# A decoder layer on one core: exponentials left unnormalised until the head output, and their high halves made by ScalarE

## The reference

```python
q = rmsnorm(x @ w_qa, q_norm_w) @ w_qb           # 16 heads, 128 + 64 rotary
kv = rmsnorm(kv_c, kv_norm_w) @ w_kvb            # 16 heads, keys and values of 128
scores = einsum('blhd,bmhd->bhlm', q, k) * scale # causal mask
attn = softmax(scores, axis=-1)
out = einsum('bhlm,bmhd->blhd', attn, v)
x = x + out.reshape(B, L, H * DV) @ w_o
```

## Time and profile before

| | us |
|---|---|
| median of 3 runs | 1166.24 (1164.35 to 1167.4) |
| profiled execution, its own time | 1167.31 |
| its span, first to last instruction | 1165.5 |
| PE busy | 957.6 (82%) |
| DVE busy | 963.2 (83%) |
| ACT busy | 643.6 (55%) |
| POOL busy | 249.7 (21%) |

### The profile page before, as it was taken

The page is one execution under the profiler, slowest core; times in us unless marked ns, Lnnn a source line. Parts: engine busy times, 40 slices in busy tenths (PEclk is TensorE's granted clock), DMA queues, the critical chain, the costliest instruction groups (busy, mean ns, idle before and its releaser), DMA issues.

```text
span 1165.5 us, 17748 instructions
## 1 busy us (share of the span) xinstructions
PE 957.6 (82%) x5622; PEld 546.8 (47%) x5640; DVE 963.2 (83%) x2902; ACT 643.6 (55%) x1437; POOL 249.7 (21%) x268
## 2 busy tenths in 40 slices
PE   0446567889999999999999999999978655559997
PEld 0324333554554555555555555555535444435553
DVE  5767748999888988998998988988968898857885
ACT  1446546666555656656656656666513675753442
POOL 1036522122112112212212212112100113221211
PEclk9769789999999999999999999999989888769999
DMA  9300004534433446443436433335364530002434
GB/s 346 145 1 1 10 8 85 93 76 80 94 67 78 81 78 154 84 74 78 88 77 151 77 70 68 68 63 136 71 212 109 146 103 6 1 0 37 80 85 91
DMA packets 247661, 98.19 MB, mean 84 GB/s; under 512 B 221832, under 2 KB 233096, under 8 KB 247056
## 3 DMA queue, kind: packets, MB, share of 16 engines
q1 hardware_dynamic: 247568, 97.06, 36.6%
HBM read 36.06 MB, written 7.34 MB: 37 GB/s over the span
## 4 chain that ended last, share of the span: by engine, by line
DVE 48%; PE 34%; ACT 7%; issue 6%; DMA 3%; POOL 2%; SPq 0%; DVEq 0%; ACTq 0%; POOLq 0%
PE bank L1964 8%; PE bank L1912 5%; DVE bank L1541 4%; DVE arena L1558 4%; PE bank L1858 4%; PE bank L1949 4%; DVE arena L1565 4%; DVE arena L797 3%; PE bank L1891 3%; DVE arena L715 2%; DVE arena L717 2%; DMA arena<-arena 2%; DVE arena L681 2%; DVE arena L1572 2%; DVE arena L1525 2%
## 5 line engine op out<-in xcount | busy, mean ns | idle before, releaser
L1241 ACT ACTIVATE arena<-bank,arena 128x128 f32<-128x128 f32 (+3 forms) x256 | 134.3, 525 | 108.2 <-DVE arena L1541 106.7
L1964 PE MATMUL bank<-arena 128*128 128x512 f16 x768 | 180.3, 383 | 1.9 <-DVE arena L1591 1.9
L1565 DVE SCALAR_TENSOR_TENSOR arena<-arena 128x128 f16<-128x128 f32 (+3 forms) x256 | 144.3, 564 | 9.1
L1541 DVE CUSTOM_DVE_ANT_0 bank<-bank,maskb,scal 128x128 f32<-128x128 f32 (+3 forms) x256 | 141.4, 552 | 12.1 <-PE bank L1937 11.6
L1949 PE MATMUL bank<-arena 128*128 128x512 f16 (+3 forms) x768 | 119.7, 308 | 33.6 <-DVE arena L1572 24.6
L1912 PE MATMUL bank<-arena 128*128 128x512 f16 x576 | 137.2, 384 | 0.0
L1949 PEld LDWEIGHTS bank<-arena 128*128 128x128 f16 x768 | 72.8, 100 | 92.9 <-issue 46.4
L1558 DVE TENSOR_SCALAR arena<-arena 128x128 f16<-128x128 f32 (+3 forms) x256 | 109.0, 426 | 7.3 <-DVE arena L1550 0.3
L1964 PEld LDWEIGHTS bank<-arena 128*128 128x128 f16 x768 | 74.0, 99 | 82.9 <-issue 6.0
L1087 POOL TENSOR_TENSOR arena<-arena 128x512 f32<-128x512 f32 x32 | 45.3, 1415 | 308.7 <-ACT arena L1261 308.5
L1261 ACT ACTIVATE arena<-bank 32x512 f32<-32x512 f32 x128 | 75.2, 588 | 30.9 <-PE bank L1891 29.6
(11 more groups left out here) (200 smaller groups left out, 1892.8 us busy)
## 6 DMA issues: line engine op xcount, KB each, us to landing
arena<-arena SPq DMA_TRANSPOSE x308, 2.7
arena<-in_L_attn_w_qb SPq DMA_DIRECT2D x1, 4608.0 KB, 21.0
arena<-in_x SPq DMA_DIRECT2D x4, 1024.0 KB, 6.0
arena<-in_L_attn_w_o SPq DMA_DIRECT2D x1, 4096.0 KB, 31.4
arena<-in_fside_BxS2xS SPq DMA_DIRECT2D x4, 1024.0 KB, 8.2
arena<-in_L_ffn_w SPq DMA_DIRECT2D x8, 512.0 KB, 7.9
out<-arena SPq DMA_DIRECT2D x16, 256.0 KB, 2.4
arena<-in_x SPq DMA_DIRECT2D x12, 256.0 KB, 2.9
```

The costliest lines, as they stand in the source:

```text
L1241: act.activation(pf(k), banks[S_BANKS[G % 3]][:, 0:n].rearrange("p (t c) -> p t c", c=P), ACT.Exp, bias=NB[:, k:k + 1], scale=-1.0, accum_ ...
L1541: dve.tensor_tensor_reduce(s, s, maskb[:, L - n:L], nsc_exp, 3e38, ALU.add, ALU.min, NB[:, (g & 3):(g & 3) + 1]).then_inc(s_max, 1)
L1565: dve.scalar_tensor_tensor(out=ph_part(k, 1), in0=pf(k), scalar=R4[:, k:k + 1], in1=ph_part(k, 0), op0=ALU.mult, op1=ALU.subtract).then_in ...
L1964: last = pe.matmul(banks[Y_BANK][:, :], ot(gp, a, k, (q & 3) * P, P), wo(b, gp * GH + k), start=(k == 0 and n == 0), stop=(k == GH - 1 and ...
```

## The change

- `exps` keeps all 8 row sums of a pair; the exponentials stay unnormalised.
- `probs_hi` moves to ScalarE, right behind `exps` of the same group, as a copy times 4096. `probs_lo` stays on VectorE.
- `row_scale` becomes one reciprocal of four columns for each head.
- The reciprocals of a head lie one per partition (the query row), while the head's output has the queries along its columns. So they are stored to DRAM (`store_sums`, 2 KB) and loaded back spread over all 128 partitions (`spread_sums`, 256 KB) on SP's queue.
- `out_norm` on VectorE multiplies the head output in PSUM by them, in place, ahead of `out_hi`.
- Two output banks, 3 and 7, by the parity of the head. `values` waits for `out_lo` of two heads earlier. The prepared tile's product, which had bank 7, now goes to bank 3.
- The orders on the engines are changed: `out_hi(2i-2)` stands behind `qn_hi_` of group 0, `out_hi(2i-1)` behind `rope_hi` (even pairs, group 5) or at group 6 (odd), and `out_lo(2i-1)` at group 6, ahead of `qn_lo_(2i+2)`, or at group 7. `prep_mm` and what hangs on it stand a group later. `values(i, 0)` waits for `cf_made` in the pairs that prepare a tile.
- `XT` shares the memory of `XN`, `square_out` that of `CF`.

```diff
+    rc_dram = nc.dram_tensor("reciprocals_of_row_sums", (B * H, P * TB), fp32, kind="Internal").ap()
...
-        XT = take(D)
+        RB = take(2 * L)
...
-        NB, SUM, RC, R4 = (small[:, 20 + 4 * k:24 + 4 * k] for k in range(4))
+        NB, SUM, RC = small[:, 20:24], small[:, 24:32], small[:, 32:40]
...
-        S_BANKS, T_BANK, O_BANK, Y_BANK, Q_BANK, R_BANK, P_BANK = (0, 1, 2), 2, 3, 4, 5, 6, 7
+        S_BANKS, O_BANKS, Y_BANK, Q_BANK, R_BANK, P_BANK = (0, 1, 2), (3, 7), 4, 5, 6, 7
...
+            return RB[:, h * L:(h + 1) * L].rearrange("p (q t) -> p t q", t=TB)
...
-                if not (n == TB):
-                    sp.wait_ge(xn_made, n)
+                sp.wait_ge(xn_lo, n)
...
+            def store_sums(Hd):
+
+                sp.wait_ge(s_rc, Hd + 1)
+                sp.dma_start(rc_dram[Hd].rearrange("(q t) -> q t", t=TB),
+                             RC[:, (Hd & 1) * TB:(Hd & 1) * TB + TB]).then_inc(rc_out[Hd & 1], 16)
+
+            def spread_sums(Hd):
+
+                sp.wait_ge(rc_out[Hd & 1], 16 * (Hd >> 1) + 16)
+                if Hd >= 2:
+                    sp.wait_ge(o_nrm, Hd - 1)
+                sp.dma_start(RB[:, (Hd & 1) * L:(Hd & 1) * L + L],
+                             rc_dram[Hd].partition_broadcast(P)).then_inc(rc_in[Hd & 1], 16)
 
             def turn_rows(n):
...
-                    if i % 2 == 0 and g == 3 and i // 2 + TB < NT:
+                    if i % 2 == 0 and g == 4 and i // 2 + TB < NT:
                         turn_keys(i // 2 + TB)
-                    if i % 2 == 0 and g == 4 and i // 2 + TB < NT:
+                    if i % 2 == 0 and g == 5 and i // 2 + TB < NT:
                         turn_latents(i // 2 + TB)
+                    if g in (3, 7):
+                        store_sums(2 * i + (g >> 2))
+                    if g == 5:
+                        spread_sums(2 * i)
+                    if g == 1 and i > 0:
+                        spread_sums(2 * i - 1)
                     turn_probs(i, g)
                     if g == 3 and i % 2 == 0 and i // 2 + 5 < NT:
                         load_xt(i // 2 + 5)
@@ -1052,6 +1082,7 @@
                         if g == 7:
                             reload_xa(i // 8)
                     if i == NPAIR - 1 and g == 7:
+                        spread_sums(2 * i + 1)
                         first_loads(sp)
             later_sync(sp)
 
...
-                    if (j, g) == (0, 2):
+                    if (j, g) == (0, 3):
                         if prep is not None:
                             prep_norm(prep[0])
-                    if (j, g) == (0, 3):
                         if not last:
...
+            def probs_hi(i, g):
+
+                k, G = g & 3, 8 * i + g
+                act.wait_ge(s_exp, G + 1)
+                if not (i == 0 and g < 4):
+                    act.wait_ge(pt_in[k], 16 * (2 * i + (g >> 2)))
+                act.activation(ph_part(k, 0), pf(k), ACT.Copy, scale=PSCALE).then_inc(s_hi, 1)
...
-                act.wait_ge(pv_mm, Hd + 1)
-                act.activation(ot(gpar, 0, slot, 0, L), banks[O_BANK][:, :], ACT.Copy).then_inc(o_hi, 1)
+                act.wait_ge(o_nrm, Hd + 1)
+                act.activation(ot(gpar, 0, slot, 0, L), banks[O_BANKS[Hd & 1]][:, :], ACT.Copy).then_inc(o_hi, 1)
...
                 for g in range(8):
                     exps(G + g, g)
+                    probs_hi(i, g)
                     if (j, g) == (0, 0):
                         qn_hi_(2 * i + 1, 1)
-                    if (j, g) == (0, 1):
+                        if not first:
+                            out_hi(2 * i - 2)
+                    if (j, g) == (0, 2):
                         if prep is not None:
                             prep_squares(prep[0])
                     if (j, g) == (0, 3):
                         if not last:
                             rope_swap(i + 1)
+                    if (j, g) == (0, 4):
                         if prep is not None:
                             prep_scale(prep[0])
-                    if (j, g) == (0, 4):
-                        if not first:
-                            out_hi(2 * i - 1)
                         if not last:
                             qn_hi_(2 * i + 2, 0)
                     if (j, g) == (0, 5):
                         if not last:
                             rope_hi(i + 1, 1 - j)
+                        if not first:
+                            out_hi(2 * i - 1)
+                    if (j, g) == (0, 6):
                         if prep is not None:
                             prep_cn(*prep)
-                    if (j, g) == (0, 7):
-                        out_hi(2 * i)
                     if (j, g) == (1, 0):
                         qn_hi_(2 * i + 1, 1)
+                        out_hi(2 * i - 2)
                     if (j, g) == (1, 2):
                         if not last:
                             rope_swap(i + 1)
                     if (j, g) == (1, 3):
                         if not last:
                             qn_hi_(2 * i + 2, 0)
-                    if (j, g) == (1, 4):
-                        if not first:
-                            out_hi(2 * i - 1)
                     if (j, g) == (1, 5):
                         if not last:
                             rope_hi(i + 1, 1 - j)
                     if (j, g) == (1, 6):
+                        out_hi(2 * i - 1)
                         if ahead is not None:
                             prep_hi(ahead)
-                    if (j, g) == (1, 7):
-                        out_hi(2 * i)
...
+            def row_scale(Hd):
+
+                h = Hd & 1
+                dve.wait_ge(s_exp, 4 * Hd + 4)
+                if Hd >= 2:
+                    dve.wait_ge(rc_out[h], 16 * (Hd >> 1))
+                dve.reciprocal(RC[:, h * TB:h * TB + TB], SUM[:, h * TB:h * TB + TB]).then_inc(s_rc, 1)
...
+                                         scalar=PSCALE, in1=ph_part(k, 0), op0=ALU.mult,
...
+            def out_norm(Hd):
+
+                h = Hd & 1
+                dve.wait_ge(pv_mm, Hd + 1)
+                dve.wait_ge(rc_in[h], 16 * (Hd >> 1) + 16)
+                o = banks[O_BANKS[h]].rearrange("p (t q) -> p t q", t=TB)
+                dve.tensor_tensor(o, o, rb(h), ALU.mult).then_inc(o_nrm, 1)
...
                     if (j, g) == (0, 0):
                         if not first:
-                            row_scale(G - 1, 7)
-                            probs_hi(i - 1, 7)
+                            row_scale(2 * i - 1)
                             probs_lo(G - 1, 7)
+                            out_norm(2 * i - 2)
+                    if (j, g) == (0, 1):
+                        probs_lo(G + 0, 0)
+                        if not first:
                             out_lo(2 * i - 2)
-                    if (j, g) == (0, 1):
-                        row_scale(G, 0)
-                        probs_hi(i, 0)
-                        probs_lo(G, 0)
                         if started(i - 5):
                             add_y(i - 5)
                         qn_lo_(2 * i + 1, 1)
                     if (j, g) == (0, 2):
-                        row_scale(G + 1, 1)
-                        probs_hi(i, 1)
                         probs_lo(G + 1, 1)
+                    if (j, g) == (0, 3):
+                        probs_lo(G + 2, 2)
                         if prep is not None:
                             prep_rope(prep[0], prep[2])
                             prep_var(prep[0])
-                    if (j, g) == (0, 3):
-                        row_scale(G + 2, 2)
-                        probs_hi(i, 2)
-                        probs_lo(G + 2, 2)
-                        if prep is not None:
-                            prep_srq(prep[0])
-                            prep_rope_sum(prep[0])
                     if (j, g) == (0, 4):
-                        row_scale(G + 3, 3)
-                        probs_hi(i, 3)
+                        row_scale(2 * i)
                         probs_lo(G + 3, 3)
                         if not last:
                             rotate(i + 1)
                         if prep is not None:
+                            prep_srq(prep[0])
+                            prep_rope_sum(prep[0])
+                    if (j, g) == (0, 5):
+                        probs_lo(G + 4, 4)
+                        if not first:
+                            out_norm(2 * i - 1)
+                        if prep is not None:
                             prep_split(prep[0])
-                    if (j, g) == (0, 5):
-                        row_scale(G + 4, 4)
+                    if (j, g) == (0, 6):
+                        probs_lo(G + 5, 5)
                         if not first:
...
-                        probs_hi(i, 4)
-                        probs_lo(G + 4, 4)
-                    if (j, g) == (0, 6):
-                        row_scale(G + 5, 5)
-                        probs_hi(i, 5)
-                        probs_lo(G + 5, 5)
```

(40 more changed lines are left out.)

47 lines of the change are left out of this document (16 added, 31 removed).

## The result

The changed kernel takes 1210.3 us (median of four runs, 1209.51 to 1211.02) against 1165.5 for the kernel before: a ratio of 1.038, interval 1.0365 to 1.0401. The forecast was 1183 us and at most 1202: the sign was right, but the loss that it forecast (17 us) was less than half of what came (45).

What follows compares the result with a forecast made beforehand. The prediction took PE as the bound, with the chain through DVE and ACT in pairs 0 to 3. Its terms summed to +17 us on the profiled 1167.3, 1184, so 1183 us for the median; range 1155 to 1202.

Steps and rivals of the forecast that it cites:

- pairs 0 to 5: First six pairs: the chain per pair about 20.5 us against 21.1, so -3 us (-8 to +2).
- pairs 6, 10, 14, 18, 22: Even pairs with a tile, index not a multiple of 4: 23.9 us each, together -2 us (-5 to +2).
- pairs 8, 12, 16, 20: Even pairs whose projection also waits for `out_lo(2i-1)`: 25.85 us each, together +4 us (0 to +8).
- pairs 24, 26, 28, 30: Late even pairs without a tile: 23.6 or 21.65 us against 19.55, together +12 us (+6 to +15).
- clock: TensorE's clock falling after stalls in pairs 8, 12, ..., 28: six chances of 1.7 us, half taken, +5 us (0 to +10).
- all outside the walk's pairs: End of the walk, where `out_norm` lengthens the last head by 0 to 2 us: +1 us.
- The chain: End of even pairs: `out_hi` behind `rope_hi`, with `out_lo` ahead of `qn_lo_`, makes the next scores wait; period 23.9 against 24.25 us.
- the old wait: `values(i, 0)` waiting for `out_lo` of the head before: a 1.8 us stall that two output banks remove.
- The shared buffers and the moved preparation steps cost nothing more: Shared memory and later preparation of a tile: no added cost, since earlier users are done a group or more before.
- by the same walk: Following an even pair's engine operations from its start in the diff's orders; applied to pairs 0 to 5: about 20.5 us.
- PE stays the bound and all stalls go: Faster rival, over the whole walk: the 24.6 us of waits and some 3 us in first pairs go, 1139 us; chance 0.16.
- The third rival: Transposes or reciprocals land late, holding up ACT's exponentials: 0.3 us for each of 64 heads, 1203 us; chance 0.10.

Runs made afterwards that it cites:

- p_pool_held: The changed kernel with only GpSimd's multiplication by the sines held, in pairs with a tile, until VectorE's key part is done: 1209.7 us, ratio 1.037.
- a_qn_first: The changed kernel with `qn_lo_(2i+2)` ahead of `out_lo(2i-1)` on VectorE in group 6 of even pairs: 1199.2 us, ratio 1.028.
- d_kr_early: The changed kernel with the tile's key part (`prep_srq`, `prep_rope_sum`) ahead of `rotate` on VectorE in group 4 of even pairs: 1179.9 us, ratio 1.012.
- o_before_tail_late: The kernel before with one part of the change: key part behind the rotation, the tile's scaling, split and turns a group later: 1182.6 us, ratio 1.015.
- g_all: The changed kernel with three swaps: key part ahead of rotation, `qn_lo_` ahead of `out_lo`, `out_hi` ahead of `rope_hi`: 1154.5 us, ratio 0.991.
- e_dense_rb: The changed kernel with `out_norm` reading the spread reciprocals without the step of four words (values wrong, same work): 1211.8 us in one execution.
- The last version: g_all with `add_y` ahead of `out_lo(2i-2)` and, in every fourth pair, `out_lo(2i-1)` ahead of `qn_lo_`, on VectorE: 1142.6 us, ratio 0.980.

## Why the prediction was half right

The account of the spans, 1165.5 to 1207.9 us, by the forecast's own terms (sums of pair periods):

| term | forecast | before | after | measured |
|---|---|---|---|---|
| pairs 0 to 5 | -3 | 127.4 | 138.0 | +10.6 |
| pairs 6, 10, 14, 18, 22 | -2 | 120.8 | 125.9 | +5.1 |
| pairs 8, 12, 16, 20 | +4 | 99.4 | 118.6 | +19.2, clock in it |
| pairs 24, 26, 28, 30 | +12 | 78.3 | 89.9 | +11.6 |
| clock | +5 | | | in the rows above, about 12 with pair 4 |
| all outside the walk's pairs | +1 | | | -4.2 |
| sum | +17 | | | +42.3 |

Of the 25.3 us between the two sums, 11.7 are 1.3 us in each of nine even pairs, 5 the clock in four of them beyond what was forecast, and 13.6 the pairs 0 to 5. What stands outside takes 5.2 away: it was 4.2 us shorter where 1 more was forecast. Most of that is the stretch from pair 31 on, 332.8 us before and 329.5 after; it varies from 329 to 333 us among the traces here, so nothing is read into it.

**What was right.** The chain. `rope_hi`, then `out_hi`, `out_lo`, `qn_lo_` took the place of the old wait. In the late even pairs, which have no tile, the forecast had 23.6 and 21.65 and they took 23.4 to 23.6 and 21.4; odd pairs stayed at 20.35; `prep_mm` starts 7.44 us into pair 18 (593.85; forecast 7.5); the reciprocals are on time. The swaps of `out_hi` and of `qn_lo_` confirm their links.

**The step that failed.** "The shared buffers and the moved preparation steps cost nothing more: the earlier users are done a group or more before." The prediction asked when the buffers come free and priced the moved instructions at nothing, without looking at what runs beside them in the new place. There GpSimd has two instructions of 1.27 us. They make row maximum 5 start at 18.62 instead of the 17.18 that p_pool_held shows for the same order undisturbed. There the exponential of group 5 begins at 17.76 and ScalarE is through its copy at 18.76 (it then idles 1.29 us for GpSimd's sum): the forecast's 18.8. Measured in the kernel after is 20.1, and these 1.3 us go through unchanged to `qn_lo_`, over at 25.11 where 23.8 was forecast. So the pairs 6, 10, 14, 18 and 22 are 25.2 and not 23.9. That the period would have been 23.9 with GpSimd out of the way and its sum in time is worked out, not measured: no run had both. The kernel before had warned of it in its own trace, where the split ran beside GpSimd's product and sum (timeline, pair 20):

```profile
620.03 1.75 POOL L1087 TENSOR_TENSOR arena<-arena 128x512 f32<-128x512 f32 x1 [3.93 <-ACT arena L1261]
...
621.92 1.26 POOL L1093 TENSOR_TENSOR arena<-arena 128x512 f32<-128x512 f32 x1
```

```profile
619.90 0.75 DVE L1565 SCALAR_TENSOR_TENSOR arena<-arena 128x512 f16<-128x512 f32 x1
...
621.17 0.90 DVE L1523 CAST arena<-arena 128x512 f16<-128x512 f32 x1
622.10 1.64 DVE L1525 TENSOR_TENSOR arena<-arena 128x512 f16<-128x512 f32 x1
```

The product takes 1.75 us instead of 1.27; VectorE's low half, which had begun first, ends at 620.65. Then the cast and the subtraction are the long ones. Moved out from beside GpSimd, these two take 0.42 and 0.69 us in the kernel after. The change exchanged who is held, and took the shorter instructions that the chain runs over.

**The clock term was mis-sized.** It priced a chance of one half at 1.7 us in six pairs, +5 in all. In pairs 8, 12, 16 and 20 the stall before `project` was 4.3 us instead of 2.95 (the same 1.3 us more), and the low clock came every time and lasted for all twelve multiplies: 2.5 us each, 10 for the four, and pair 4, at 29.4 us, is like them. 25.85 + 1.3 + 2.5 is 29.65, as measured. The price was half of 3.4 us, which is how long the low clock of the earlier trace rows lasted (202.8 to 206.2); behind the longer stalls the granted clock stayed low for 6.8 us (559.3 to 566.1 in pair 16). In pairs 24 and 28, where TensorE idled 2.9 and 3.1 us before the projection, the clock stayed full, and the term was worth nothing. That was luck: in a_qn_first and d_kr_early pair 24 has the same stall of 2.9 us, the clock fell behind it, and the pair takes 25.1 us instead of 23.4, the forecast's 1.7 us more. That the length of one stall doesn't settle it shows within d_kr_early as well: TensorE idles 2.54 us before the projection in pairs 8, 12, 16 and 20 alike. Behind two of these stalls (windows of pair 12 and of pair 16) the clock was

```profile
446.20:450.40 4.20, 4.17 (x12) 1.57 (x13) 1.71 (x4) 2.22 (x5) 0.00 (x0) 0.62 0.58 116
537.40:539.90 2.50, 2.50 (x12) 1.18 (x13) 1.67 (x4) 1.95 (x5) 0.00 (x0) 1.00 0.32 60
```

0.62 and 1.00: it fell in two of the four pairs. In o_before_tail_late it fell behind six of nine stalls of the same length. So one half is about right for these. Behind the stalls of 4.3 us it fell every time, in a_qn_first too, though there in three of five for a part of the twelve multiplies only (0.58 to 0.61 over them). There is no edge in length of the kind that the prediction read from the earlier trace rows: behind 3.1 us (pair 28) the clock stayed full in all five kernels that have this stall.

**Pairs 0 to 5** were called 20.5 us in the mean "by the same walk" and took 23.0. The walk was not made for them. Pair 4 has a projection that waits for `out_lo(2i-1)` as pairs 8 to 20 have, and the forecast left it out of them: it takes 29.4 us instead of 22.7, 6.7 of the 10.6 us. Pair 2 carries the tile's chain and ends in a drawn wait of 4.75 us for `qn_lo_` (25.0 instead of 21.65), and pair 0 in one of 3.96 us for the rope's high half (22.9 instead of 21.6). With the key part early (d_kr_early) the six take 128.8 us, in g_all 123.2 (127.4 before). So the -3 was there to be had, in another order.

**`out_norm`** was priced at 0.69 us with 0.9 as its upper end, from the nearest row by operand places and not by steps; it takes 1.075. By e_dense_rb's one execution that moved nothing here.

**The rivals.** "PE stays the bound and all stalls go, 1139 us" named its own condition, `out_lo(2i-1)` over by 20.3 and `qn_lo_` by 22.0. The last version meets it (20.4 and 19.8 in pair 18) and comes to 1142.6 us: the price was right, and the orders decide which side one lands on. The third rival, late landings, did not come, though its 1203 us was the nearest number: that is chance.

What stays open: what decides whether the clock falls behind one of several equal stalls. Nor was a version tried in which GpSimd's two instructions are out of VectorE's way and its sum still comes in time.

## What to carry to other kernels

When an instruction is moved in a queue, look in the trace at what every other engine runs in its new place, and price it from a row that has the same neighbour; an operation of 0.26 us became one of 1.27. Moving work to an idle engine decided little by itself here (to have the copies on ScalarE changed nothing in one order and gained 6 us in the other); the order within each in-order queue, against the chain that the next stage waits for, was worth 56 us with the same work. And a stall of TensorE that grows can be paid twice, once as itself and once more in the multiplies behind it: 4.3 and 2.5 us here.

## What the runs showed of the hardware that was not expected

- VectorE's scales of 2 and 64 columns on arena data took 0.64 and 1.27 us beside GpSimd's products of 1.28 and 1.27 us, each ending with them, and 0.22 and 0.25 without. It seems to work in both directions: in the kernel before GpSimd's product took 1.75 us behind a low half of VectorE that had begun first. A rotation with one input in PSUM wasn't held.
- VectorE's multiplication of a bank of 512 fp32 columns by an arena row took 1.075 us with the row read at a step of four fp32 words, and 0.690 without the step.
- After stalls of 4.3 us the granted clock was 0.50 over the next twelve multiplies (5.3 us for 2.75), five times in five in the kernel after. Behind shorter, equal stalls it fell sometimes: after 2.54 us twice in five (pairs 4 to 20 of d_kr_early) and six times in nine (o_before_tail_late), after 2.9 us in two of five (pair 24 of a_qn_first and d_kr_early, not of the kernel after, e_dense_rb and p_pool_held), and after 3.1 us in none of five (pair 28 of the same).
